# Blocks that are not needed read the first expert's places, and the experts' end zeros are issued two ticks after the table's

## The reference, cut to what matters

```
x = x + 0.5 * ffn(layernorm(x))      # stage 1: the change is here
x = x + attention(layernorm(x))      # local windows of 64, and 256 chosen tokens per row
x = x + 0.5 * ffn(layernorm(x))      # stage 3: the same ffn and weights

def ffn(x):                           # 8 experts, 256 -> 128 -> 256
    w = softmax(x @ router_w + router_b)          # per token
    top, which = top_k(w, 2);  top = top / sum(top)
    h = gelu(x @ W1[e] + b1[e])                   # for each expert e
    return sum over e of (h @ W2[e] + b2[e]) * (share of e, 0 where e is not among the two)
```

## Time and profile before

| what | us |
|---|---|
| median of 3 runs | 2088.14 (2086.48 to 2088.15) |
| the profiled execution | 2087.82 |
| its span in the profile | 2086.0 |
| PE busy | 1875.4 (90%) |
| DVE busy | 1387.4 (67%) |
| ACT busy | 1205.9 (58%) |
| POOL busy | 1175.2 (56%) |

### The profile page before, as it was taken

The page is one execution under the profiler, slowest core; times in us unless marked ns, Lnnn a source line. Parts: engine busy times, 40 slices in busy tenths (PEclk is TensorE's granted clock), DMA queues, the critical chain, the costliest instruction groups (busy, mean ns, idle before and its releaser), DMA issues.

```text
span 2086.0 us, 38095 instructions
## 1 busy us (share of the span) xinstructions
PE 1875.4 (90%) x11764; PEld 1398.7 (67%) x11764; DVE 1387.4 (67%) x4768; ACT 1205.9 (58%) x2974; POOL 1175.2 (56%) x1356
## 2 busy tenths in 40 slices
PE   3388889689989989989989998998999899999998
PEld 1166678456666666666666666666676688888887
DVE  4354445755775775775775775775754488888887
ACT  6376657456566566566566565566555555555554
POOL 3997862373583583583584584484453444444443
PEclk8699999899999999999999999999999999999999
DMA  8578787110220220220220220220112111111110
GB/s 273 203 234 324 272 299 254 60 52 1 78 56 6 74 57 8 74 57 9 74 57 9 72 56 11 67 60 12 34 41 105 38 41 41 41 41 41 32 40 22
DMA packets 106577, 173.65 MB, mean 83 GB/s; under 512 B 13297, under 2 KB 64905, under 8 KB 105481
## 3 DMA queue, kind: packets, MB, share of 16 engines
q1 hardware_dynamic: 83336, 118.42, 17.1%
q0 software_dynamic: 20736, 52.52, 8.1%
q10 hardware_dynamic: 2304, 0.28, 0.1%
HBM read 80.33 MB, written 90.84 MB: 82 GB/s over the span
## 4 chain that ended last, share of the span: by engine, by line
PE 51%; DVE 16%; POOL 11%; issue 10%; ACT 9%; DMA 3%; SPq 1%; ACTq 0%; DVEq 0%; POOLq 0%
PE bank L723 7%; PE bank L725 6%; PE bank L724 6%; PE bank L1012 5%; PE bank L1001 4%; PE bank L972 4%; PE bank L983 4%; PE bank L943 3%; PE bank L880 2%; ACT prob L1309 2%; POOL prob L1989 2%; PE bank L865 2%; DVE x L1578 2%; POOL spots_d L1936 2%; DVE st L1402 2%
## 5 line engine op out<-in xcount | busy, mean ns | idle before, releaser
L1989 POOL TENSOR_TENSOR prob<-prob,rden 128x512 f32<-128x512 f32 x320 | 337.2, 1055 | 447.8 <-DVE rden L1784 444.2
L1309 ACT ACTIVATE prob<-prob,nmax 128x256 f32<-128x256 f32 x512 | 255.9, 502 | 399.1 <-DVE nmax L1766 390.3
L1766 DVE CUSTOM_DVE_ANT_0 prob<-bank,mask 128x256 f32<-128x256 f32 x512 | 195.5, 418 | 102.8 <-PE bank L972 101.7
L1653 DVE SCALAR_TENSOR_TENSOR xb<-bank,gate,xb 128x256 f32<-128x256 f32 x512 | 211.8, 476 | 58.1 <-PE bank L725 57.6
L972 PE MATMUL bank<-kT,qT 64*128 64x256 f32 x1024 | 212.0, 433 | 22.9 <-DVE nmax L1766 22.4
L1916 POOL TENSOR_TENSOR hl<-hf,hh 128x512 fp32r<-128x512 f32 x128 | 164.9, 1294 | 115.1 <-ACT hh L1112 110.6
L983 PE MATMUL bank<-ident,prob 128*128 128x128 f32 x1280 | 198.4, 278 | 22.4 <-POOL prob L1989 22.4
L983 PEld LDWEIGHTS bank<-ident,prob 128*128 128x128 f32 x1280 | 153.1, 141 | 81.5 <-POOL prob L1989 35.3
L1778 DVE COPY probT<-bank 128x512 f32<-128x512 f32 x160 | 110.1, 688 | 116.8 <-PE bank L983 115.9
L1111 ACT ACTIVATE hf<-bank,b1s 128x512 f32<-128x512 f32 x128 | 88.2, 689 | 171.9 <-PE bank L725 168.6
L1001 PE MATMUL bank<-probT,V 128*64 128x128 f32 x2048 | 169.7, 287 | 8.7 <-ACT oT_s L1325 7.7
(11 more groups left out here) (255 smaller groups left out, 5047.5 us busy)
## 6 DMA issues: line engine op xcount, KB each, us to landing
xin<-spots_d SPq DMA_DIRECT2D x85, 256.0 KB
made_d<-yout SPq DMA_DIRECT2D x85, 256.0 KB
x<-in_L_attn_x SPq DMA_DIRECT2D x8, 1024.0 KB
x_d<-x SPq DMA_DIRECT2D x8, 1024.0 KB, 4.5
xb<-x_d SPq DMA_DIRECT2D x16, 512.0 KB, 3.8
out<-xb SPq DMA_DIRECT2D x16, 512.0 KB, 3.0
xb<-in_L_attn_x SPq DMA_DIRECT2D x7, 1024.0 KB, 6.9
spots_d<-zeros SPq DMA_DIRECT2D x24, 256.0 KB
```

What stands on the lines that cost most here:

```text
L1309: act.activation(prob[j % NP][:, h, :], src, ACT.Exp, bias=nmax[:, j % 4, h:h + 1], scale=-1.0 if light else 1.0, accum_out=den[:, j % 4, ...
L1653: dve.scalar_tensor_tensor(out=x, in0=bank[ob][:, (t % 2) * D:(t % 2 + 1) * D], scalar=gate[:, k % 2, t, e:e + 1], in1=x, op0=ALU.mult, op ...
L1766: ins = dve.tensor_tensor_reduce(prob[j % NP][:, h, :], bank[g % NS][:, 0:KEYS], mask[:, which, :], -1.0, 3e38, ALU.add, ALU.min, nmax[:, ...
L1989: pool.tensor_tensor(prob[j % NP][:, :, :], prob[j % NP][:, :, :], rden[:, j % 4, :].unsqueeze(2).broadcast_to([P, 2, KEYS]), ALU.mult).th ...
```

## The change

- The seven spare zero blocks per batch, the three DMAs of 1792 KB that wrote them and the waits for them are gone.
- The table's last step becomes two. The first computes each block's first place as before, as fp32; the second multiplies it by (`passed` of the last expert < 0.5), which is 1 for a block that is needed and 0 for the others. Those read place 0, which is the first expert's first block.
- `pads(n)` is no longer part of the first `block_load`. Its eight DMAs are issued in two halves, in ticks +12 and +13 of the batch's last row: SP's ticks 18 and 19, 38 and 39, 65 and 66.

```diff
-        spots_d = [... [SPARE[n] + (E - 1) * BLK, D] ...]
+        spots_d = [... [SPARE[n], D] ...]
-        NA, NPOS, NTAB = 11, 6, 16
+        NA, NPOS, NTAB = 11, 6, 17
-            def pads(n):
+            def pads(n, i):
+                if n == 0 and i == 0:
+                    sp.wait_ge(s_const, CONST)
                 sp.wait_ge(s_tab, NTAB * (n + 1))
-                for e in range(E):
+                for e in range(E // 2 * i, E // 2 * (i + 1)):
                     row = value(sp, pad_row[n][0:1, e:e + 1], 0, SPARE[n] - BLK)
                     sp.dma_start(spots_d[n][bass.ds(row, BLK), :]..., zeros[:, :, :]).then_inc(s_zero, 16)
             def block_load(s_):
                 n = batch_of(s_)
                 if s_ == FIRST[n]:
-                    pads(n)
                     sent(sp, n)
                     sp.wait_ge(s_zero, 16 * E * (n + 1))
-                    sp.wait_ge(s_spare, 16 * (n + 1))
...
                 for r in row_at(tau + 5, 0):
                     if r >= 4:
                         row_load(r)
+                for i in range(2):
+                    for r in row_at(tau, 12 + i):
+                        if last_of_batch(r):
+                            pads(batch_of_row(r), i)
...
-                if tau in (12, 40, 64):
-                    if tau == 12:
-                        sp.wait_ge(s_const, CONST)
-                    n = (12, 40, 64).index(tau)
-                    sp.dma_start(spots_d[n][SPARE[n]:SPARE[n] + (E - 1) * BLK, :]..., zeros ...).then_inc(s_spare, 16)
...
-                dve.scalar_tensor_tensor(out=block_row[b][:, 0:nb], in0=block_f[:, 1, 0:nb], scalar=base_f[:, 0:1], in1=i_blk[:, 0:nb], op0=ALU.add, op1=ALU.add).then_inc(s_tab)
+                dve.scalar_tensor_tensor(out=block_f[:, 1, 0:nb], in0=block_f[:, 1, 0:nb], scalar=base_f[:, 0:1], in1=i_blk[:, 0:nb], op0=ALU.add, op1=ALU.add).then_inc(s_tab)
+                dve.wait_ge(s_tab, n + 16)
+
+                dve.scalar_tensor_tensor(out=block_row[b][:, 0:nb], in0=passed[:, 0:nb, E - 1], scalar=0.5, in1=block_f[:, 1, 0:nb], op0=ALU.is_lt, op1=ALU.mult).then_inc(s_tab)
```

More of the change, by code:

```diff
@@ L257, in build @@
         made_d = [nc.dram_tensor(f"made_d{n}", [BLOCKS[n] * BLK, D], F32, kind="Internal").ap() for n in range(len(BATCH))]
-        spots_d = [nc.dram_tensor(f"spots_d{n}", [SPARE[n] + (E - 1) * BLK, D], F32, kind="Internal").ap() for n in range(len(BATCH))]
+        spots_d = [nc.dram_tensor(f"spots_d{n}", [SPARE[n], D], F32, kind="Internal").ap() for n in range(len(BATCH))]
         x2_d = [nc.dram_tensor(f"x2_d{b}", [N, D], F32, kind="Internal").ap() for b in range(ROWS)]
@@ L284, in build @@
         s_bT, s_bx, s_w1c, s_bh = sem("block_turned"), sem("block_x"), sem("w1_copied"), sem("block_hidden")
-        s_bge, s_bo, s_by, s_spare = sem("block_gelu"), sem("block_out"), sem("block_y"), sem("spare_zero")
+        s_bge, s_bo, s_by = sem("block_gelu"), sem("block_out"), sem("block_y")
         s_got, s_comb, s_xhalo = [sem(f"got{i}") for i in range(2 * T)], sem("combined"), sem("xt_halo")
@@ L599, in block_load @@
                 if s_ == FIRST[n]:
-                    pads(n)
                     sent(sp, n)
                     sp.wait_ge(s_zero, 16 * E * (n + 1))
-                    sp.wait_ge(s_spare, 16 * (n + 1))
                 if s_ >= 4:
                     sp.wait_ge(s_bT, s_ - 3)
-                row = value(sp, block_row[n][0:1, s_ - FIRST[n]:s_ - FIRST[n] + 1], 0, SPARE[n] + (E - 2) * BLK)
+                row = value(sp, block_row[n][0:1, s_ - FIRST[n]:s_ - FIRST[n] + 1], 0, SPARE[n] - BLK)
                 sp.dma_start(xin[s_ % 4][:, :, :], spots_d[n][bass.ds(row, BLK), :].rearrange("(p s) d -> p s d", s=BT)).then_inc(s_bld[s_ % 4], 16)
@@ L649, in sp_program @@
                     sp.dma_start(b2_all[:, :, :].rearrange("p e n -> p (e n)"), b2.rearrange("(a e) n -> a (e n)", a=1).broadcast_to([P, E * D])).then_inc(s_b2all, 16)
-                if tau in (12, 40, 64):
-                    if tau == 12:
-                        sp.wait_ge(s_const, CONST)
-                    n = (12, 40, 64).index(tau)
-                    sp.dma_start(spots_d[n][SPARE[n]:SPARE[n] + (E - 1) * BLK, :].rearrange("(j p s) d -> p j (s d)", p=P, s=BT),
-                                 zeros[:, :, :].rearrange("p s d -> p (s d)").unsqueeze(1).broadcast_to([P, E - 1, BT * D])).then_inc(s_spare, 16)
                 if tau == 18:
@@ L1248, in evac @@
                         act.wait_ge(s_zero, 16 * E * len(BATCH))
-                        act.wait_ge(s_spare, 16 * len(BATCH))
                     if 4 * x + i > 1:
@@ L2040, in pool_program @@
                     pool.wait_ge(s_zero, 16 * E * len(BATCH))
-                    pool.wait_ge(s_spare, 16 * len(BATCH))
                     for part in xt:
```

## The result

The changed kernel takes 2082.55 us (median of 22 runs, 2073.78 to 2089.18), the kernel before 2091.18 us (22 runs, 2086.48 to 2096.27). The ratio is 0.996, with a 95% interval from 0.9948 to 0.9972: faster by 8.4 us, the ratio times the time before. The forecast was 2075, between 2067 and 2083, that is a gain of 12.9 us.

What follows compares the result with a forecast made beforehand. It took stage 1's PE waits for block loads held up by late zeros as the bound: −4.3 − 10.6 + 3.0 + 0.6 − 1.6 = −12.9 us, giving 2075 us, range 2067 to 2083.

Steps and rivals of the forecast that it cites:

- First batch, nothing: First batch's load waits for the last send of tokens; its zeros were hidden and stay so: 0 us.
- Second batch, −4.3: Second batch's first load then waits for the last send alone, going out 4.46 us earlier: gain 4.3 us, between 2.0 and 6.0.
- 8 us for a load that takes some 3 us: Behind ticks 38 and 39, block 19's load has 8 us before its turn, so holding SP costs nothing.
- Third batch, −10.6: Third batch's first block: 8.67 us PE wait and half-speed matmuls after it go, a gain of 10.57 us.
- Moved zeros there, +3: Ticks 65 and 66: held SP costs PE 1 us, zeros' bytes 2.8; 3 us taken, between 0 and 7.5.
- a reserve of 4.7 us: Third batch's zeros: block 46's load goes out 5.7 us late against this slack, leaving PE 1 us late.
- My formula: Ticks 65 and 66: 9 × (297 + 233 − 405) = 1.1 MB left over, delaying transfers behind by 2.8 us.
- Table +0.6: One more table step on DVE costs 0.3 us in each of the second and third batch.
- fetches −1.6: POOL's fetches for row 0 start some 5 us earlier, removing PE's 1.49 us hold and a slower matmul: gain 1.6 us.
- Spare zeros removed, 0 or "some back": Spare blocks reading tokens cost 0; the missing 1.8 MB spare DMA near tick 64 gives back some of the moved zeros' cost.
- rival C: Stage 1 stalls mostly replaced, as stores and loads stand behind SP's zeros: gain 4.5 us, time 2083.6; chance 0.21.
- POOL's wait under 4 us: Sign in the changed profile: POOL's wait ahead of its memset, 14.25 us before, should be under 4 us.

Runs made afterwards that it cites:

- experiment 1: Changed kernel with the eight zeros put back at each batch's first load, so only the spare zeros are removed: 2087.74 us, ratio 0.9956 to the kernel before.
- experiment 3: Changed kernel with the second and third batch's zeros spread, one or two per tick instead of four and four: 2083.25 us, ratio 0.9924 to the kernel before.
- e9_after_x: Changed kernel with row 0's 1 MB load for the attention in tick 64 instead of 74: 2085.92 us, ratio 0.9959 to the kernel before.
- experiment 6: Kernel of experiment 1 plus one 1 MB DMA of zeros to an unused tensor in ticks 38, 39, 65, 66: 2092.37 us, ratio 1.0004 to the kernel before.
- experiment 2: Kernel before with the zeros moved as in the changed kernel, but the spare-zero DMAs kept: 2096.17 us, ratio 0.9993 to the kernel before.
- experiment 5: Kernel of experiment 1 plus four 16-row DMAs, at places read from the table, in ticks 38, 39, 65, 66: 2091.14 us, ratio 0.9991 to the kernel before.
- experiment 4: Kernel of experiment 1 plus four 16-row DMAs, at fixed places, in ticks 38, 39, 65, 66: 2088.76 us, ratio 0.9979 to the kernel before.

## Why the prediction was right and where it was wrong

The time lies in the range, 7.5 us above the value named, and the sign is right. The sum was not, and that the range was met is in part luck. Of 12.9 us forecast for stage 1 its profiles show 3.0, or 3.7 from the span's start; some 5 us of the measured 8.4 come from where the forecast had nothing and are not placed. The forecast was also counted from 2088.14 us, the median of three runs, where 22 give 2091.18; that is 3.0 of the 7.5 us. By its own steps:

- **First batch, nothing: right.** The load goes 91.19 − 88.28 = 2.91 us after the last send, as before, with zeros issued by 70.5.
- **Second batch, −4.3: wrong, +1.1.** This is the step that failed. The stall itself went: no wait for the batch's first load is left. But "8 us for a load that takes some 3 us" priced the load of block 19 by the earlier trace rows, by loads that had little ahead of them, and left out row 6's 1 MB, which SP issues in the same tick 39. Behind that and 2 MB of zeros it took 8.49 us. It went out at 160.62, 2.6 us later than said, and PE waited 3.40 us and ran at half speed behind it. Neither does it alone: in experiment 1 row 6's load is there without the zeros, and PE doesn't wait at block 19; in experiment 3 the load took 10.34 us but went out sooner, and PE waited 0.60. No run moves row 6's load. The removed spare DMA did not cancel this by standing "in the same place": experiment 1 gives 2.5 us for its absence, and the moved zeros take 3.7 over experiment 1, although that kernel still has 1.97 us of the stall.
- **Third batch, −10.6: right in mechanism, −9.7 measured.** The missing part is the row's 1 MB load ahead of block 54's; without it (e9_after_x) the column is 11.5 us shorter.
- **Moved zeros there, +3: mis-sized, +6.5** (7.0 against experiment 1). Both parts were named and both were low: the hold 1 us against 2.8, the bytes 2.8 against 5.0 where they come in whole MBs (experiment 6), or 4.3 as what is left of the 7.0. For the hold I gave PE a reserve of 4.7 us, as if SP's issues took as long behind the zeros as elsewhere and only a load were waited for; but SP took 11.7 us for two loads, and DVE's wait of 5.83 us for a store in the same queue shows a second customer. That DVE's wait cost anything is not shown. For the bytes I took 405 GB/s as what the DMA engines reach; with the mix of transfers here, a full share is less, as the window of the changed kernel shows:

```profile
255.00:260.00 5.00, 3.44 (x17) 2.49 (x15) 0.69 (x1) 2.57 (x6) 4.50 (x7) 1.00 0.99 341
```

  A share of 0.99 gives 341 GB/s here. My formula with 341 gives 9 × (297 + 233 − 341) = 1.7 MB left over, and 5.0 us at that rate, the cost that experiment 6 measured. That is worked out after the fact and not shown; experiment 6's own zeros, in larger pieces, ran at 387 GB/s in one such window (250 to 255). The estimate of about 5 us from the Trainium skill's limit of HBM ("DMA: Bandwidth & Descriptors", Specifications) is nearer to the 7.0 than my 3.8; 1.5 MB at 358 GB/s are 4.3 us, and the hold's 1 us comes to it. Its reason isn't borne out by the traces, since the changed kernel too exceeds 358 GB/s, in the window that follows the second batch's zeros and row 6's load:

```profile
165.00:170.00 5.00, 1.60 (x13) 1.41 (x13) 1.44 (x4) 0.89 (x2) 4.51 (x7) 0.82 1.06 410
```

  The same page's rule that DMAs of all engines interleave on the same 16 (Issuing engines are not separate DMA queues), which I cited against the move, fits experiment 6; as SP issues the zeros, loads and stores alike, no run here separates that from SP's own order.
- **Table +0.6, fetches −1.6:** "56–84", where the fetches are, is 1.0 us shorter, and PE's wait of 1.49 us is gone. The second and third batch's tables are made in "0–15" and "26–42", which differ by +0.3 and −0.3 us. Each of these is below what a profile tells.
- **Spare zeros removed, 0 or "some back": wrong.** In stage 1 their absence is worth 3.3 us with the zeros in the old place, and 5.4 us with the zeros moved.

The mechanism is that of rival C (0.21), stalls mostly replaced through the queue, with bytes as well as the held SP behind it. Its time, 2083.6, was nearer too, and its gain of 4.5 us is near the 3.0 to 3.7 of stage 1.

Of the signs named, POOL's wait under 4 us, no wait at the second batch's first block and full speed behind the third's came true. The third batch's first block still waits 1.16 us, the new wait ahead of it, at block 46, ends at 262.25 and not before 256, the chain at the second batch goes by block 19's load and not by the last send, and the attention begins 3.7 us earlier and not 13.

**What stays open.** The runs gain 8.4 us, the profiles of stage 1 only 3.0. For experiment 1 it is 9.2 and 3.3, and for experiment 2, where the profile loses 2.4 us, the runs gain 1.5. Behind stage 1 the profiles don't show 5 us that belong to the change. From the first output store to the end it is 406.3 to 406.9 us in all. The stretch before, from the attention's first matmul, takes 1318.8 us on average in the nine profiles without the spare zeros and 1322.2 in the five with them, but 1315.2 to 1322.2 and 1317.4 to 1326.9 overlap. So those 5 us are not placed. Nor was it tried to issue the zeros from another engine, which would tell SP's order from the load on the DMA engines as such, or to leave out the experts' end zeros, since loads would then read places that nobody wrote.

## What to carry to other kernels

A DMA moved to where its wait is hidden still stands in a queue: look at what is behind it there, and price those transfers by a row that had bytes ahead of it, not by the quickest load of the trace, and list every transfer in that stretch, the large reads too. Spread a large write over many steps, so that the issuing engine comes to each load sooner and fewer bytes are ahead of it; here that was worth 4.6 us in one batch and 4.5 in the other. When a stall goes, check the transfers that it had been hiding, as the row's 1 MB load here.

## What the runs showed of the hardware

- A block's load of 256 KB takes 2.70 to 3.02 us with little ahead of it. Issued 2 to 7 us behind the 1 MB load of a row in the same queue it took 8.49 and 8.63 us in the changed kernel and 10.34 and 9.30 in experiment 3, with or without zeros in between. With only zeros ahead, 1 MB of them issued over 3.5 us, block 46's load took 3.44 us: it was late by its issue. With each MB of zeros in one DMA, a load 10 us behind took 6.33 us (experiment 6).
- Where the place comes from a table, four or eight DMAs in a row held SP for 0.73 to 1.16 us each, the reading of the place included (four took 2.93 us in experiment 5, and 4.62 in the changed kernel behind the store of the weights); with a fixed place it was 0.46 to 0.53 us (experiment 4: 1.84 and 2.12 for four). Issuing a plain store took 0.33 us on a quiet stretch and 1.66 with 2 MB of zeros issued 7 to 10 us before (experiment 6).
- A full DMA share stood for quite different rates: 405 GB/s at 1.05 and 341 at 0.99 in the changed kernel.
- Equal programs differ by 9 us in one stretch of some 1320 us. Spells of lower granted clock, 0.83 in one stretch of 10 us against 1.00, fall differently in them, but the mean clock sets only the longest apart (0.979 against 0.986 and 0.987).
